# Two layers of a Mamba block gated by a mixture of experts: predicated copies for the first layer's expert, silu in groups of four on ScalarE in the second

## The chip, the cores and the metric

The kernel runs on one core of one Trainium2 chip. The time is device microseconds of one launch. The core has five engines that run side by side and meet at semaphores: TensorE (PE; its weight loads are PEld), VectorE (DVE), ScalarE (ACT), GpSimd (POOL) and SyncE (SP), which here issues all the DMAs.

## The reference, cut to what matters

Input x is 8 x 256 x 128. Both layers compute x = x + s(xn) * silu(ffn(xn)), where xn is the layer norm of x.

```python
# layer 0: ffn, top-1 of 8 experts, each 128 -> 512 -> 128
#   p = softmax(xn @ Wr + br); e = argmax(p)      (for each token)
#   y = p[e] * (relu(ln(xn) @ W1[e] + b1[e]) @ W2[e] + b2[e])
# layer 1: ffn, all 8 experts, weighted
h = jax.nn.silu(x @ w_gate[e]) * (x @ w_up[e])
out = sum_e cw[e] * (h @ w_down[e])   # cw: product of two softmaxes, normalised
# s: Mamba. xc = conv(x @ W_in); gate = silu(xc) (layer 0: times z)
#   delta = softplus(... + b);  state = exp(delta * A) * state + (delta * u) * B;  y = sum_n state * C
# layer 1: y = (y + xc * D) * silu(z) @ W_out, 256 inner channels, 16 states
```

## The kernel before

The 2048 tokens are four pairs of sequences, T = 512 tokens each; a pair goes through layer 0, then (all four done) through layer 1. Tiles are 128 partitions (channels) by 512 tokens, fp32.

A pair has 32 *units* (8 experts x 4 slices of 128 hidden channels), and its work is cut into 32 *slots*, one for each unit. Every engine's program is written out in the order of slots; a loop over pairs runs from slot 6 of one pair to slot 5 of the next, so slots 0 to 5 also hold the *late* part of the pair before. The engines are not otherwise tied: each walks through its own list and waits for semaphores. In a slot stand:

- the unit. `three_passes` forms a hidden tile in one of two PSUM banks (bank2, bank3) out of a high and a low part of weights and input (L1384 to L1386). Layer 0: `hidden0` adds a fourth product, `big` (2^100 on a diagonal, bf16) times `ohm` (one-hot minus 1) at L1426, so that tokens of other experts come out hugely negative; ScalarE's relu with bias (`rectify`, L1186) makes them zero; `down0` (L1444) adds every unit into bank1, two slots later. Layer 1: ScalarE takes tanh of half the gate (`half_gate`, L1225), VectorE multiplies (tanh + 1) by the gate (`finish_gate`, L739, tile gg), TensorE's `up1` (L1496) fills the single bank5 a slot later, VectorE multiplies both (`finish_hidden`, L747, tile hid), and `down1` (L1504) follows three slots later. Before its up product, TensorE waits for the hidden step that frees bank5;
- a *chunk*: one of 16 (layer 0) or 32 (layer 1) state indices. ScalarE forms decay = exp(delta * A) (L1179, ring of four), VectorE drive = dx * B (L612) and the scan over tokens (`tensor_tensor_scan`, L619), POOL multiplies by C and adds (L898 to L923), TensorE sums with the identity (L1397, L1405). B and C come as rows broadcast over partitions by DMA (tile CB, ring of four), each loaded when POOL is done with the chunk four back;
- steps of the *head* of the next pair, given by the tables `HEAD0` and `HEAD1` (slot: names). Each engine has its own part of a step: stat1, var1 and xn are the layer norm, xnT its transposes on TensorE and their copy on ScalarE (L1116), xi0 and xi1 the convolution products (L1359), xs0 and xs1 their silu, z and tz/sz the gate of the block, row and dt the products for B, C and delta, then softplus in parts (ln is a Ln with a table load on each side, L1146 and L1147), lmax, lexp, pick or soft the routing, cwT the experts' weights. All head products share bank7, and each waits until the one before has been read;
- the tail of layer 0's own pair (`TAIL0`): y, yn1, yn2, yn, ynT, s in slots 27 to 31.

In the late part layer 0 adds the experts' biases (L1485), copies bank1 (L1213), transposes it and takes silu of it by tanh (L1218, L673). In the last pair of layer 0 the head is layer 1's, and the gate weights of layer 1 are loaded and split.

The lines that set the order around the change:

```python
CHUNKS1 = [c if c < 8 else c - 1 for c in range(C1)]      # slot of each chunk's drive; scan one slot later
half_gate(i, u)                                            # ACT, every slot
gate1(i, u + 1) ; down1(i, u - LAG1) ; up1(i, u - 1)       # PE, every slot
scan ; finish_hidden(i, u - 2) ; form_drive ; finish_gate  # DVE, every slot
```

## Time and profile before

| | us |
|---|---|
| median of 3 runs | 913.11 (912.3 to 918.16) |
| profiled execution | 914.93, span 913.1, granted TensorE clock 0.971 |
| TensorE busy | 805.6 (88%) |
| VectorE busy | 682.9 (75%) |
| POOL busy | 490.3 (54%) |
| ScalarE busy | 420.7 (46%) |

The span goes from the first to the last instruction of the profiled execution. Busy shares are means over both layers: layer 0 fills the span up to about 400 us, layer 1 the rest. Records of matmuls overlap, so that TensorE's busy time is more than its work; the distance between the starts of two products tells what one costs. In the timelines "x2" is two instructions of one fp32 product.

### The profile page before, as it was taken

The page shows a single profiled execution, that of the slowest core. Times are in us where ns is not written, and L with a number is a line of the kernel's source. Part 1 is how long each engine was busy: PE and PEld are TensorE (multiplying, and loading weights), DVE is VectorE, ACT ScalarE, POOL GpSimd, SP SyncE. Part 2 cuts the span into 40 slices and gives each one's busy share as a digit, 9 for nine tenths or more (in the row PEclk, how much of TensorE's full clock was granted, in tenths as well). Part 3 has the DMA queues.
Part 4 walks back from the last instruction along what each step waited for, and adds up shares of the span by engine and source line. Part 5 has one row for each costly group of instructions (what it writes and reads, how often), then busy time and mean ns, then how long its engine had stood idle before and what let it go on. Part 6 is the DMA issues. An engine that isn't in the chain of part 4 may idle for free.

```text
span 913.1 us, 10705 instructions
## 1 busy us (share of the span) xinstructions
PE 805.6 (88%) x2312; PEld 383.6 (42%) x2312; DVE 682.9 (75%) x1096; ACT 420.7 (46%) x699; POOL 490.3 (54%) x388
## 2 busy tenths in 40 slices
PE   2858998999899988868998987999887999889997
PEld 1324444444444443333454343544343544344443
DVE  4389359927973845349879897789896889899995
ACT  2744554455455634555334633434542434563341
POOL 0086436634660553225756656656655656757773
PEclk9979999999999989998999999999998999999999
DMA  9265255332523553167744575756565745758771
GB/s 266 57 189 136 89 169 150 104 106 83 161 54 106 150 169 88 31 162 193 186 146 125 131 186 143 187 128 154 143 154 131 178 132 141 176 138 212 189 186 35
DMA packets 85851, 129.28 MB, mean 142 GB/s; under 512 B 7368, under 2 KB 28560, under 8 KB 85808
## 3 DMA queue, kind: packets, MB, share of 16 engines
q1 hardware_dynamic: 85808, 128.85, 53.7%
q14 instruction: 33, 0.27, 0.1%
q8 instruction: 10, 0.16, 0.1%
HBM read 125.35 MB, written 3.47 MB: 141 GB/s over the span
## 4 chain that ended last, share of the span: by engine, by line
PE 30%; DVE 16%; issue 11%; ACT 4%; DMA 3%; POOL 1%; DVEq 1%; SPq 1%; ACTq 0%; POOLq 0%
DVE state L619 6%; PE bank L1496 6%; PE bank L1504 5%; DVE bank L612 3%; PE bank L1359 3%; PE bank L1397 3%; DMA CB<-crow 3%; PE bank L1384 2%; PE bank L1386 2%; PE bank L1444 2%; PE bank L1385 2%; DVE gg L739 2%; PE bank L1314 1%; DVE hid L747 1%; ACT sg L1225 1%
## 5 line engine op out<-in xcount | busy, mean ns | idle before, releaser
L619 DVE TENSOR_TENSOR_SCAN state<-decay,bank 128x512 f32<-128x512 f32 x192 | 232.9, 1213 | 17.5 <-issue 9.1
L1384 PE MATMUL bank<-XH,wh 128*128 128x512 f32 x256 | 176.3, 689 | 25.5 <-DVE gg L739 11.1
L1496 PE MATMUL bank<-xw,wu 128*128 128x512 f32 x256 | 141.9, 637 | 36.5 <-DVE hid L747 36.2
L1179 ACT ACTIVATE decay<-delta,negA 128x510 f32<-128x510 f32 x192 | 135.7, 715 | 42.0 <-DVE state L619 41.7
L1186 ACT ACTIVATE hid<-bank,early 128x512 f32<-128x512 f32 x128 | 87.5, 685 | 142.0 <-PE bank L1444 132.2
L612 DVE TENSOR_TENSOR bank<-bank,CB 128x512 f32<-128x512 f32 x192 | 133.2, 694 | 20.6 <-DMA CB<-crow 11.5
L1444 PE MATMUL bank<-hid,wd 128*128 128x512 f32 x256 | 147.5, 659 | 0.0
L902 POOL TENSOR_TENSOR product<-state,CB 128x512 f32<-128x512 f32 x64 | 81.7, 1276 | 99.9 <-DVE state L619 99.9
L1504 PE MATMUL bank<-hid,wd 128*128 128x512 f32 x256 | 132.4, 600 | 0.0
L1225 ACT ACTIVATE sg<-bank 128x512 f32<-128x512 f32 x128 | 75.7, 592 | 99.9 <-PE bank L1386 99.9
L898 POOL TENSOR_TENSOR product<-state,CB 128x512 f32<-128x512 f32 x64 | 81.6, 1276 | 74.4 <-DVE state L619 44.4
L739 DVE SCALAR_TENSOR_TENSOR gg<-sg,bank 128x512 f32<-128x512 f32 x128 | 86.8, 678 | 36.4 <-ACT sg L1225 36.2
L1386 PE MATMUL bank<-XH,wl 128*128 128x512 f32 x256 | 103.5, 404 | 0.0
L1385 PE MATMUL bank<-XL,wh 128*128 128x512 f32 x256 | 102.8, 402 | 0.0
L1384 PEld LDWEIGHTS bank<-XH,wh 128*128 128x128 f32 x256 | 49.6, 194 | 113.5 <-DVE gg L739 52.5
L1496 PEld LDWEIGHTS bank<-xw,wu 128*128 128x128 f32 x256 | 44.1, 194 | 120.9 <-DVE hid L747 94.0
L919 POOL TENSOR_TENSOR product<-state,CB 128x512 f32<-128x512 f32 x48 | 61.4, 1280 | 61.9 <-DVE state L619 57.6
L747 DVE TENSOR_TENSOR hid<-gg,bank 128x512 f32<-128x512 f32 x128 | 84.7, 662 | 5.9 <-PE bank L1496 3.7
L904 POOL TENSOR_TENSOR product<-product 128x512 f32<-128x512 f32 x64 | 83.7, 1307 | 5.0
L1385 PEld LDWEIGHTS bank<-XL,wh 128*128 128x128 f32 x256 | 49.8, 194 | 37.5 <-issue 36.5
L923 POOL TENSOR_TENSOR product<-product 128x512 f32<-128x512 f32 x48 | 63.2, 1317 | 3.8
L1397 PE MATMUL bank<-product,early 128*128 128x512 f32 x128 | 64.7, 592 | 0.0
(167 smaller groups left out, 922.6 us busy)
## 6 DMA issues: line engine op xcount, KB each, us to landing
CB<-crow SPq DMA_DIRECT2D x256, 256.0 KB, 5.0
CB<-crow SPq DMA_DIRECT2D x64, 512.0 KB, 4.8
cwb<-cwrow SPq DMA_DIRECT2D x32, 256.0 KB, 5.7
wu<-W_dram SPq DMA_DIRECT2D x8, 256.0 KB, 5.3
wd<-W_dram SPq DMA_DIRECT2D x8, 256.0 KB, 5.9
wu<-Wu_dram SPq DMA_DIRECT2D x8, 256.0 KB, 3.6
xw<-Wg_dram SPq DMA_DIRECT2D x8, 256.0 KB, 4.6
wd<-Wd_dram SPq DMA_DIRECT2D x8, 256.0 KB, 5.0
```

Source lines behind the costliest of these rows:

```text
L612: v.tensor_tensor(drive, dx, CB[:, c % ROWS, 1, :], ALU.mult).then_inc(drive_ready.sem, 1)
L619: v.tensor_tensor_scan(state[:, c % RING, :], decay[:, c % RING, :], drive, 0.0, ALU.mult, ALU.add).then_inc(state_ready.sem, 1)
L739: v.scalar_tensor_tensor(out=gg[:, u % 2, :], in0=sg[:, u % 2, :], scalar=1.0, in1=bank[HID_BANK + u % HIDS][:, :], op0=ALU.add, op1=ALU.m ...
L747: v.tensor_tensor(hid[:, u % 2, :], gg[:, u % 2, :], bank[UP_BANK][:, :], ALU.mult).then_inc(hid_ready.sem, 1)
L1179: a.activation(by_batch(decay[:, c % RING, :])[:, :, 1:], by_batch(delta[:, m, :])[:, :, 1:], ACT.Exp, scale=negA[:, c:c + 1]).then_inc(de ...
L1384: t.matmul(dst, wh[:, e, ws], XH[:, :], start=True, stop=False)
L1385: t.matmul(dst, wh[:, e, ws], XL[:, :], start=False, stop=False)
L1386: return t.matmul(dst, wl[:, e, ws], XH[:, :], start=False, stop=stop)
L1397: t.matmul(bank[Y_BANK][:, :], ident[:, :], product[:, e % PRODS, :], start=(k == 0), stop=(k == N // PAIR - 1)).then_inc(summed.sem, 1)
L1444: t.matmul(bank[OUT_BANK][:, :], wd[:, u, :], hid[:, u % 2, :], start=(u == 0), stop=False).then_inc(down_done.sem, 1)
L1496: t.matmul(bank[UP_BANK][:, :], wu[:, e, 128 * f:128 * f + 128], xw[:, e % 2, :], start=True, stop=True).then_inc(up_ps.sem, 1)
L1504: ins = t.matmul(bank[OUT_BANK][:, :], wd[:, u, :], hid[:, u % 2, :], start=(u == 0), stop=(u == UNITS - 1))
```

## The change

Layer 0. The mask product and `ohm` go. Each expert's four down products now form a sum of their own, in bank5 and bank1 by turns, and when an expert's sum is complete VectorE copies it into `yfT` where a mask says that the token is this expert's (`select`, 8 for each pair, in slots 6, 10, ... 30 and slot 2 of the next pair). The masks are the one-hot rows, written to DRAM (`send_mask`, in slot 18) and loaded back broadcast over the partitions (`load_mask`). Bias product and transposes of the late part are joined; the transposes of yn go to bank6.

Layer 1. ScalarE computes silu itself, in a group of four units at every fourth slot, with its table loaded before it and the exponentials' table after it; then the exponentials of the scans of slots 4e+3 to 4e+6. Decay and silu tiles lie in rings of six. TensorE computes the gates two by two, in the first and the last slot of a group. VectorE's `finish_gate`, and its steps for xs and sz, go. `HEAD1` is laid out anew, and hand-over, low part, delta and the first two decays of the next pair move from its slot 0 into slots 29 to 31 of the pair before.

```diff
-HEAD1 = {... 11: "xnT", 12: "xi0", 13: "logits", 14: "lmax", 15: "lexp",
-         16: "xs0 z0 tz0", 17: "sz0 xi1", 19: "xs1", 20: "row0", 21: "z1 tz1 soft1", 22: "sz1",
-         24: "dt0 soft2", 25: "row1 rest0 soft3", 26: "dt1 less0", 27: "cwT rest1", 28: "less1 ln", 29: "xr"}
+HEAD1 = {... 11: "xnT", 12: "logits", 13: "lmax", 14: "xi0 lexp",
+         16: "xs0 z0 sz0", 17: "row0", 18: "xi1 soft1", 20: "xs1 z1 sz1", 21: "row1 soft2", 22: "dt0 soft3",
+         23: "rest0", 25: "dt1 less0 rest1", 26: "cwT less1", 29: "ln hand xr", 30: "low del0", 31: "dec0"}
+DECAYS1 = [[c for c in range(2, C1) if FT * e + 3 <= SCAN1[c] <= FT * e + 6] for e in range(E)]
+PLACE = [k % SIX for k in range(UNITS - FT)] + [0, 1, 4, 5]
...
+            def load_mask(j, e):
+                if j > 0 or e >= CWR:
+                    sp.wait_ge(sel_ready.sem, sel_ready.at0(j, e - CWR + 1))
+                src = cwrow[j % 2, e:e + 1, :].to_broadcast((128, T))
+                sp.dma_start(cwb[:, e % CWR, :], src).then_inc(cw_in[e % CWR].sem, 16)
+            def send_mask(j):
+                sp.wait_ge(*use0(head_read, j, "onehot"))
+                sp.dma_start(cwrow[j % 2, :, :], ohT[:, :]).then_inc(cw_out.sem, 16)
+                sp.wait_ge(cw_out.sem, cw_out.at0(j, 16))
...
-                v.tensor_scalar(ohm[:, :], ohT[:, :], 1.0, None, ALU.subtract).then_inc(ohm_ready.sem, 1)
+            def select(i, e):
+                dve.wait_ge(cw_in[e % CWR].sem, cw_in[e % CWR].at0(i, 16 * (e // CWR + 1)))
+                dve.wait_ge(down_done.sem, down_done.at0(i, FT * e + FT))
+                dve.wait_ge(sel_ready.sem, sel_ready.at0(i, e))
...
+                v.memset(pause[:, e % 2:e % 2 + 1], 0.0)
+                v.copy_predicated(yfT[:, :], cwb[:, e % CWR, :].bitcast(mybir.dt.int32), bank[out_bank(e)][:, :]).then_inc(sel_ready.sem, 1)
...
-            def finish_gate(i, u):
-                v.scalar_tensor_tensor(out=gg[:, u % 2, :], in0=sg[:, u % 2, :], scalar=1.0, in1=bank[HID_BANK + u % HIDS][:, :],
-                                       op0=ALU.add, op1=ALU.mult).then_inc(gg_ready.sem, 1)
-                v.tensor_tensor(hid[:, u % 2, :], gg[:, u % 2, :], bank[UP_BANK][:, :], ALU.mult).then_inc(hid_ready.sem, 1)
+                v.tensor_tensor(hid[:, u % 2, :], sg[:, PLACE[u], :], bank[UP_BANK][:, :], ALU.mult).then_inc(hid_ready.sem, 1)
...
-                half_gate(i, u)
...
+                if u % FT == 0:
+                    silu(i, u)
+                    silu(i, u + 1)
+                    for name in steps_:
+                        if name in ("xs0", "xs1"):
+                            head(name, j)
+                    silu(i, u + 2)
+                    silu(i, u + 3)
...
+                    for c in DECAYS1[u // FT]:
+                        form_decay(i, c)
...
-                three_passes(dst, e, f, False)
-                t.matmul(dst, big[:, e:e + 1].to_broadcast((E, 128)), ohm[:, :], start=False, stop=True).then_inc(hid_ps.sem, 1)
+                three_passes(dst, e, f, True).then_inc(hid_ps.sem, 1)
...
-                t.matmul(bank[OUT_BANK][:, :], wd[:, u, :], hid[:, u % 2, :], start=(u == 0), stop=False).then_inc(down_done.sem, 1)
+                t.matmul(bank[out_bank(e)][:, :], wd[:, u, :], hid[:, u % 2, :], start=(f == 0), stop=(f == FT - 1)).then_inc(down_done.sem, 1)
...
-                if u + 1 < UNITS:
+                if u % FT == 0:
+                    gate1(i, u + 2)
+                    gate1(i, u + 3)
+                if u % FT == FT - 1 and u + 1 < UNITS:
                     gate1(i, u + 1)
+                    gate1(i, u + 2)
```

ScalarE in layer 1 before, from the copy of the transposed input (slot 11) over slot 12; sg is the tanh of a gate, sp_u and sp_l are xi0's two readings:

```order
L1116 ACTIVATE XNP<-bank7 128x2x256 [waits xl_ready,xr_ready]
L1222 REGISTER_ALU
L1224 REGISTER_ALU [waits hid_ps]
L1225 ACTIVATE sg<-bank2 128x512 [waits gg_ready]
L1178 REGISTER_ALU [waits delta_ready]
L1179 ACTIVATE decay<-delta,negA1 128x2x255 [waits state_ready]
L1118 REGISTER_ALU
L1119 ISA [waits head_ps]
L1122 ACTIVATE sp_u<-bank7,early 128x512 [waits delta_ready,sp_l_ready,xs_ready]
L1123 ACTIVATE sp_l<-bank7,early 128x512
```

The same place now (sg is silu):

```order
L1153 ACTIVATE XNP<-bank7 128x2x256 [waits xl_ready,xr_ready]
L1265 REGISTER_ALU
L1267 REGISTER_ALU [waits hid_ps]
L1268 ACT_TABLE_LOAD
L1268 ACTIVATE sg<-bank2 128x512 [waits hid_ready]
L1265 REGISTER_ALU
L1268 ACTIVATE sg<-bank3 128x512 [waits hid_ready,hid_ps]
...
L1218 REGISTER_ALU [waits delta_ready]
L1219 ACT_TABLE_LOAD
L1219 ACTIVATE decay<-delta,negA1 128x2x255 [waits state_ready]
```

One tanh and one exponential a slot have become four silus and up to four exponentials at every fourth slot, with a table load ahead of each kind; here both stand behind the copy of the transposes.

VectorE in layer 0 before, slot 6 from the scan to the first statistics:

```order
L618 REGISTER_ALU [waits drive_ready,decay_ready]
L619 SCALAR_TENSOR_TENSOR state<-decay,bank4 128x512 [waits state_used]
L638 REGISTER_ALU
L639 COPY szm<-ohT 8x512 [waits mix_ps]
L641 TENSOR_SCALAR hp<-linv 128x4
L534 ISA
L500 BN_STATS stats<-xt 128x6 [waits x_in]
```

And now; cwb is the mask, bank5 the sum of expert 0:

```order
L669 REGISTER_ALU [waits drive_ready,decay_ready]
L670 SCALAR_TENSOR_TENSOR state<-decay,bank4 128x512 [waits state_used]
L637 ISA
L638 ISA [waits cw_in0]
L639 ISA [waits down_done]
L641 REGISTER_ALU [waits sel_ready]
L642 MEMSET pause 128x1 [waits yf_ps]
L643 COPY_PREDICATED yfT<-cwb,bank5 128x512
L693 COPY szm<-ohT 8x512 [waits yf_ps]
L695 TENSOR_SCALAR hp<-linv 128x4
L579 ISA
L545 BN_STATS stats<-xt 128x6 [waits x_in]
```

The copy, with its wait for the mask's DMA and for TensorE's fourth down product, stands ahead of the head's statistics, and one like it at every fourth slot.

TensorE in layer 0, two units before:

```order
L1384 MATMUL bank2<-XH,wh 128x512 [waits hid_ready]
L1385 MATMUL bank2<-XL,wh 128x512
L1386 MATMUL bank2<-XH,wl 128x512
L1426 MATMUL bank2<-ohm,big 128x512
L1444 MATMUL bank1<-hid,wd 128x512 [waits hid_ready,wd_in1]
L1422 REGISTER_ALU
L1384 MATMUL bank3<-XH,wh 128x512 [waits hid_ready]
L1385 MATMUL bank3<-XL,wh 128x512
L1386 MATMUL bank3<-XH,wl 128x512
L1426 MATMUL bank3<-ohm,big 128x512
L1444 MATMUL bank1<-hid,wd 128x512 [waits hid_ready]
```

and now:

```order
L1432 MATMUL bank2<-XH,wh 128x512 [waits hid_ready]
L1433 MATMUL bank2<-XL,wh 128x512
L1434 MATMUL bank2<-XH,wl 128x512
L1487 ISA [waits wd_in1]
L1489 MATMUL bank1<-hid,wd 128x512 [waits hid_ready,sel_ready]
L1470 REGISTER_ALU
L1432 MATMUL bank3<-XH,wh 128x512 [waits hid_ready]
L1433 MATMUL bank3<-XL,wh 128x512
L1434 MATMUL bank3<-XH,wl 128x512
L1489 MATMUL bank1<-hid,wd 128x512 [waits hid_ready]
```

The mask product is gone from every unit, and an expert's first down product waits for the copy of the expert two before, whose bank it takes.

## Rows read from the trace of the kernel before

**Rows 1.** The page, busy time of each engine.
```profile
PE 805.6 (88%) x2312; PEld 383.6 (42%) x2312; DVE 682.9 (75%) x1096; ACT 420.7 (46%) x699; POOL 490.3 (54%) x388
```

**Rows 2.** Stretches: us, busy PE, PEld, DVE, ACT, POOL; layer 0 (1, 3), layer 1.
```profile
125.70:210.20 84.50, 81.04 (x250) 38.19 (x250) 57.79 (x104) 44.27 (x71) 41.89 (x33) 0.98 0.38 110
294.80:403.10 108.30, 95.63 (x275) 44.07 (x275) 56.00 (x95) 54.40 (x91) 41.94 (x33) 0.94 0.39 110
529.50:661.40 131.90, 117.84 (x329) 57.31 (x329) 111.24 (x165) 57.98 (x99) 79.96 (x63) 0.97 0.62 152
791.60:895.60 104.00, 97.69 (x276) 48.24 (x276) 100.85 (x138) 41.86 (x70) 75.48 (x60) 1.00 0.74 180
```

**Rows 3.** Timeline of TensorE, layer 1: start, us, engine, line, operation, tiles.
```profile
577.64 0.39 PE L1385 MATMUL bank<-XL,wh 128*128 128x512 f32 x1
...
578.10 1.02 PE L1504 MATMUL bank<-hid,wd 128*128 128x512 f32 x2
578.96 1.02 PE L1496 MATMUL bank<-xw,wu 128*128 128x512 f32 x2
```

**Rows 4.** Timeline of VectorE over the same slot.
```profile
576.71 1.22 DVE L619 TENSOR_TENSOR_SCAN state<-decay,bank 128x512 f32<-128x512 f32 x1
...
578.42 0.69 DVE L612 TENSOR_TENSOR bank<-bank,CB 128x512 f32<-128x512 f32 x1
579.02 0.68 DVE L739 SCALAR_TENSOR_TENSOR gg<-sg,bank 128x512 f32<-128x512 f32 x1
579.61 1.21 DVE L619 TENSOR_TENSOR_SCAN state<-decay,bank 128x512 f32<-128x512 f32 x1
```

**Rows 5.** Chain that ended last, layer 1, pair 1: start, us, what.
```profile
544.69 1.79 PE bank L1541 x16
...
590.39 1.69 PE bank L1367 x16
```

**Rows 6.** Timeline of TensorE, layer 1, with [idle before <-releaser].
```profile
559.14 2.08 PE L1496 MATMUL bank<-xw,wu 128*128 128x512 f32 x2 [3.65 <-DVE hid L747]
...
656.76 0.50 PE L1384 MATMUL bank<-XH,wh 128*128 128x512 f32 x1 [1.29 <-DVE gg L739]
```

**Rows 7.** Timeline of TensorE, layer 0, a slot with nothing beside the unit.
```profile
140.10 1.12 PE L1444 MATMUL bank<-hid,wd 128*128 128x512 f32 x2
...
141.53 0.40 PE L1386 MATMUL bank<-XH,wl 128*128 128x512 f32 x1
141.86 0.39 PE L1426 MATMUL bank<-ohm,big 8*128 8x512 bf16 x1
142.18 1.13 PE L1444 MATMUL bank<-hid,wd 128*128 128x512 f32 x2
```

**Rows 8.** Busy time by stretch, layer 0, pair 1, slots 4 to 20.
```profile
137.40:183.90 46.50, 43.59 (x133) 20.49 (x132) 43.66 (x75) 22.12 (x36) 29.72 (x24) 0.96 0.45 123
```

**Rows 9.** Timelines, layer 0, pair 1: g, TensorE's wait for xn, yn.
```profile
136.87 0.69 DVE L673 SCALAR_TENSOR_TENSOR yfT<-yfT,bank 128x512 f32<-128x512 f32 x1 [3.04 <-ACT yfT L1218]
...
154.87 0.66 PE L1309 MATMUL bank<-early,xn 128*128 128x128 f32 x4 [2.42 <-DVE xn L513]
...
201.93 1.36 DVE L513 TENSOR_SCALAR so<-bank,mv,rstd_t 128x128 f32<-128x128 f32 x4 [1.20 <-POOL rstd_t L869]
```

**Rows 10.** Timeline of ScalarE around its Ln, layer 1.
```profile
519.64 1.28 ACT L1146 ACT_TABLE_LOAD   x1
520.94 1.06 ACT L1146 ACTIVATE sp_l<-sp_u 128x1024 f32<-128x1024 f32 x1
522.01 1.28 ACT L1147 ACT_TABLE_LOAD   x1
...
523.42 0.58 ACT L1225 ACTIVATE sg<-bank 128x512 f32<-128x512 f32 x1
```

**Rows 11.** The page, DMA issues: tiles, count, KB each, us to landing.
```profile
CB<-crow SPq DMA_DIRECT2D x256, 256.0 KB, 5.0
```

**Rows 12.** Groups by line: busy us, mean ns | idle before, releaser.
```profile
L747 DVE TENSOR_TENSOR hid<-gg,bank 128x512 f32<-128x512 f32 x128 | 84.7, 662 | 5.9 <-PE bank L1496 3.7 <-PE bank L1504 2.2
```

More of the change, by code:

```diff
@@ L45 @@
 RING = 4
+SIX = 6
 HIDS = 2
@@ L50 @@
 LAG0, LAG1 = 2, 3
+SELECT_AT = FT + LAG0
 GROUP = 4
@@ L123, with freed @@
 BANK1 = [s for s in steps(HEAD1) if s in "xnT xi0 xi1 logits z0 z1 cwT row0 dt0 row1 dt1".split()]
+def freed(k, pair):
+    earlier = [n for n in range(k) if PLACE[n] == PLACE[k]]
+    if earlier:
+        return max(earlier) + 1
+    if isinstance(pair, int) and pair == 0:
+        return 0
+    return max(n for n in range(UNITS) if PLACE[n] == PLACE[k]) + 1 - UNITS
 class Signal:
@@ L728, in head1 @@
                     rounding(m, sp_u_ready.at1(j, m + 1))
+                if name == "low":
+                    if not first_pair(j):
+                        low1(j)
+                if name == "del0":
+                    form_delta(lambda signal, n: signal.at1(j, n), 0, J1, decay_ready.at1(j, 0 if first_pair(j) else -N))
             def low1(i):
@@ L1144, in head1 @@
                 if name == "ln":
-                    act.wait_ge(sp_u_ready.sem, sp_u_ready.at1(j, J1))
+                    act.wait_ge(sp_c_ready.sem, sp_c_ready.at1(j, J1))
                     a.activation(sp_l[:, :, :], sp_u[:, :, :], ACT.Ln).then_inc(sp_l_ready.sem, 1)
                     a.activation(warm[:, :], ones[:, :], ACT.Exp)
+                if name == "hand" and not first_pair(j):
+                    hand_over1(j)
+                if name == "dec0":
+                    for c in range(2):
+                        form_decay(j, c)
                 if name in ("dt0", "dt1"):
@@ L1245, in slot1 @@
                     keep(i)
-                if head:
-                    for name in now(HEAD1, u):
+                for name in steps_:
+                    if name not in ("xs0", "xs1", "sz0", "sz1"):
                         head(name, j)
@@ L1482, in late0 @@
                     down0(i, UNITS - LAG0 + u)
[L1483 removed]
+                if u == 3:
+                    pe.wait_ge(sel_ready.sem, sel_ready.at0(i, E))
                     pe.wait_ge(ohF_ready.sem, ohF_ready.at0(i, 1))
[L1485 to L1487 removed]
+                    pe.wait_ge(head_read.sem, head_read.at0(PAIRS, 0) + len(BANK1) if i is PAIRS - 1 else head_read.at0(i + 2, 0))
+                    for k in range(TT):
+                        here = slice(128 * k, 128 * k + 128)
+                        t.matmul(hb[:, here], yfT[:, here], ident[:, :], start=True, stop=False)
+                        last = t.matmul(hb[:, here], ohF[:, here], b2[:, :], start=False, stop=True)
+                    last.then_inc(yf_ps.sem, 1)
             def up1(i, u):
```

205 lines of the change are left out of this document (101 added, 104 removed).

## The prediction

> **What bounds the kernel now.** I read the busy shares first, then the table of stretches, then the two timelines of TensorE and VectorE side by side, and the waits last.
>
> TensorE is busy 88% of the span and VectorE 75% [rows 1], but the two layers differ. One pair of layer 0 takes 84.5 us with VectorE busy 57.8 of them; one pair of layer 1 takes 131.9 us with VectorE busy 111.2 [rows 2]. Busy time of TensorE is inflated by overlapping records, so I use the distance between starts: an fp32 product of 512 columns costs 0.86 us (578.10 to 578.96) and one of the three gate passes 0.23 us (577.64 to 578.10 is two) [rows 3]. A unit of layer 1 is thus 3 x 0.23 + 0.86 (up) + 0.86 (down) = 2.41 us, plus a sum of 0.86 every second unit: 2.84 us. In the same slot VectorE goes scan, hidden, drive, gate: scan to scan is 2.90 us (576.71 to 579.61) [rows 4]. So the two engines are equally loaded, each waits in turn for the other, and whatever the head of the next pair adds to one of them is paid in full. A pair of layer 1 holds, on TensorE: 32 x 2.41 = 77.1; 16 sums x 0.86 = 13.8; the head's 14 large fp32 products x 0.86 = 12.0; logits 1.7 and output projection 1.8 [rows 5]; three sets of transposes, about 1.3: in all 107.7 us. Observed 131.9, so 24 us are loss: waits for VectorE (up to 3.65 us at once, and 1.29 for the gate) and the half clock after the long one, where two halves took 2.08 us and not 1.02 [rows 6, 3].
>
> In layer 0 a unit with nothing beside it takes 2.08 us (140.10 to 142.18) [rows 7]: from the third pass to the down product 0.65 (141.53 to 142.18), where layer 1 has 0.23, and about 0.1 more behind the down product. Without the mask product I expect layer 1's 0.69 + 0.86 = 1.55. But from slot 4 to slot 20 VectorE is busy 43.7 of 46.5 us [rows 8], and TensorE waits 2.42 us there for xn [rows 9]: in half of each layer-0 pair VectorE is the bound.
>
> **Layer 1, part by part.** Removed on VectorE: 32 gate steps whose pitch is 0.59 (579.02 to 579.61 [rows 4]) = 19 us of a pair, and four steps for xs and sz, some 3. VectorE's slot falls from 2.90 to 2.31, under TensorE's 2.84. TensorE becomes the only bound. The gates now come two slots together (both at a group's first and last slot), so TensorE's distances between two up products are 3.96, 1.72, 2.58, 3.10 us. In the 1.72 gap VectorE finishes its hidden step late by 0.6 us, but the next gap of 2.58 takes that up; I cost it at nothing, and at 0.6 x 8 = 5 us a pair if it does not.
>
> Added on ScalarE: 16 table loads a pair. The load starts at 519.64, the Ln behind it at 520.94, the next load at 522.01 as that Ln ends [rows 10]: 1.30 us each, 20.8 a pair. ScalarE was busy 58.0 of 131.9 [rows 2]; less the two steps for each of xi0 and xi1 (four of 0.7, 2.8) it comes to 76, of some 122. It is covered as long as it comes to a group's first silu in time: TensorE computes that gate a slot early and has 2.4 to 3.3 us of gate, down, up (and sum) before it needs the bank again, against 1.30 + 0.6 (523.42 [rows 10]) on ScalarE. The cover is missing where a head step stands directly ahead: xnT in slot 11, copied by ScalarE only after TensorE's last product of the slot, then a load, then silu(12): 0.1 + 0.6 + 1.3 + 0.6 = 2.6 us in which TensorE stands. The softplus of dt0 before silu(24) and hand-over, low and gate at slots 29 to 31 I put at 1 us each. Behind each late silu stand the decays, row and dt copies on ScalarE; the scans need the decays three slots later, which hides them. CB loads take 5.0 us to land [rows 11] in a ring of four; after row1 the loads are queued on SP behind its two writes, and with faster slots I allow 1 us.
>
> The sum for a pair with a head: 107.7 + 5.4 (the stop near 559 with its slow clock [rows 6]; it falls where the loop over pairs jumps back, and I let it stay) + 1.7 (a second slow stretch) + 2.6 + 2 + 1 + about 3 of small gaps = 123.4, against 131.9: 8.5 less, three times, 25.5. The last pair has no head: 104.0 us for its 32 slots [rows 2], of which TensorE needs 93; with 5 of small losses 98, 6 less. Its tail after the last scan stays. Layer 1: -31.5.
>
> **What the Trainium skill says of the loads.** "ScalarE: Activation LUTs", section "What ACT_TABLE_LOAD costs", gives about 1.28 us for the load and about 1.38 us of drain, 2.66 in all for a switch. The trace disagrees: the Ln began 0.02 us after its load ended and the load 0.01 us after the work before it [rows 10]. By the page ScalarE would carry 22 us more a pair, some 98 of 122, and the second rival below would be likely; by the row it has room.
>
> **Layer 0, part by part.** Removed on TensorE: 0.52 us x 32 = 16.7 a pair. Added on VectorE: 8 copies. The trace has no predicated copy. The nearest row by its operands (one in PSUM, one in SBUF) is hidden, 0.66 us [rows 12]; the dearest 512-column step is the scan, 1.21 [rows 4]. I take 0.7 with 0.1 for the memset and the waits in front, and keep 0.5 to 1.3 for the range. Also gone: the step for ohm, 0.3.
> Slots 0 to 18, VectorE's half: its wait of 3.04 us for g in slot 4 [rows 9] shrinks by 2.2, as TensorE arrives 4 x 0.52 sooner; three copies ahead of the expert choice cost 2.4; ohm gives 0.3. About nothing is gained (-0.1), and TensorE's gift of 0.52 a slot becomes a longer wait at xnT.
> Slots 19 to 31, TensorE's half: 13 x 0.52 = 6.8 less. The copy of expert 6 stands before yn in slot 30 and waits for a product of slot 29: 0.7 + 1.4 (yn [rows 9]) + 0.1 against a slot of 1.55 gives back 0.7; the chain y, stats, variance, yn, which has three slots of 1.55 instead of 2.08, I cost at 0.3: -5.8. The mask's DMAs (8 x 256 KB a pair) are queued on SP between the CB loads, and wait for a copy two experts back, which VectorE has passed by then; the one wait that blocks SP, the landing of the mask rows in slot 18, comes after the last CB load of the pair. I cost them at nothing; 1 us a pair if they delay CB.
> Pairs 1 and 2: -5.9 each. Pair 0 -4.5 (irregular start, and the first mask row is queued before the first rows). Pair 3 took 108.3 us [rows 2] and carries layer 1's first head: 20 slots behind xnT x 0.52 = -10.4, -0.6 before it, and +4.5 for four table loads in it, which hold up relu, on which TensorE waits with only 0.6 us of slack. Together -6.5. Layer 0: -22.8.
>
> **Sum.** -31.5 - 22.8 = -54.3 us. The profiled execution took 914.9 us (span 913.1 and 1.8 around it), so 860.6; the median of the runs shown is 1.8 lower: 859.
>
> **The rivals.**
> A. Layer 0 gives little: the predicated copy costs 1.2 or more, and the copies tie VectorE to TensorE. Then its half grows by 3 x 0.5, the tail by 0.5, pair 3's head by 3: layer 0 gives -12 and not -22.8. For it: VectorE's 43.7 of 46.5 us. Against: in the other half it is nearly idle. Time 870; with small losses in layer 1 up to 880.
> B. ScalarE becomes the bound in the head groups: each load costs twice the row (the page's price), the six groups with head steps of a pair lose 1.5 to 2 us each, about 11 x 3 = 33 us. Time 892. Against: the rows of the four loads show no such gap.
> C. Layer 1 gains more: the small gaps and the second slow stretch go with VectorE's waits, pairs at 116 us: 3 x 7 less. Time 838.
> D. Slower than before: TensorE waits at every group for silu. The place is the first silu of a group, behind the decays of the group before, each of which waits for the scan six chunks back. If ScalarE arrives after its whole train (4 decays x 0.6 + 2 loads x 1.3 = 5.0 us) while TensorE has 2.4 of other work, 2.6 us are lost in each of 32 groups, 83 us: 859 + 83 = 942. It decides from 1.7 us a group on (54 / 32). Against: the scan waited for is that of the group's first slot, done before the silus are.
>
> **How the numbers follow.** The forecast (845 to 869) has 0.47, A 0.20, B 0.10, C 0.16, D 0.07. The low end of the range is C, 838; the high end has to hold A and most of B, 892; what is left out is half of C's outer side, D and a little of B. A measurement of this kernel tells about 1% from no change. Faster by over 1% hold the forecast, A, C and nearly all of B: 0.90; within 1%: 0.04, slower: 0.06, from D and its milder forms.
>
> **What would show it.** In the changed trace: VectorE busy below 90 us of a layer-1 pair and pairs of about 123 us; silu groups with two loads of 1.28 each and ScalarE near 76 us a pair; TensorE waiting for ScalarE at slot 12 and hardly elsewhere; the predicated copy near 0.7 us; layer-0 pairs of 78 to 79 us with a longer wait at xnT than 2.42. The prediction is wrong if TensorE waits for silu in groups without head steps, if layer-1 pairs stay at 130, or if the layer-0 pair loses all of 16 us (then VectorE was no bound there).

## The result and the profile after

The changed kernel takes 924.13 us (median of 13 runs), the kernel before, on the same chip, 915.0 (13 runs): ratio 1.0086, 95% interval 1.0059 to 1.0114. I had forecast 859 in a range of 838 to 892. The profiled execution took 922.94 us (span 921.1). Two of the changed kernel's 13 executions (933.0 and 933.9 us) fell in a slower state of the chip and do not enter the ratio; the median of the other eleven is 923.0. The change did what it says on VectorE and ScalarE, and the time did not fall: it rose by 0.9%.

The busy times answer to [rows 1]:

```profile
PE 769.3 (84%) x2224; PEld 411.0 (45%) x2224; DVE 626.4 (68%) x1013; ACT 506.3 (55%) x755; POOL 485.3 (53%) x388
```

TensorE has 36 us less, VectorE 57 us less, ScalarE 86 us more. Now the table of stretches (us, busy PE, PEld, DVE, ACT, POOL, granted clock, DMA share, GB/s), which answers to [rows 2]: layer 0 pairs 1 and 3, then layer 1 pair 1 and the last pair.

```profile
125.00:210.00 85.00, 71.99 (x229) 42.08 (x228) 63.92 (x119) 43.45 (x70) 41.87 (x33) 0.90 0.47 138
295.00:403.00 108.00, 85.13 (x256) 47.00 (x257) 60.38 (x108) 60.05 (x95) 42.35 (x34) 0.91 0.47 132
527.60:665.20 137.60, 119.48 (x328) 60.74 (x328) 92.13 (x128) 79.17 (x115) 78.71 (x62) 0.94 0.58 144
802.00:906.00 104.00, 98.46 (x278) 51.10 (x278) 86.70 (x107) 63.48 (x86) 75.07 (x59) 0.98 0.71 178
```

The third line runs from one low part (tile XL) of layer 1 to the next, one whole period of the order. VectorE fell from 111 to 92 us in such a pair and ScalarE stands at 79, both within 3 us of the forecast; the pair lasts 137.6 us, where it lasted 131.9. The clock column moved too: 0.98 became 0.90 in layer 0, 0.97 became 0.94 in layer 1.

**Layer 0.** Timelines of VectorE, TensorE and ScalarE at the start of pair 1 (start, us, engine, line, operation, tiles, [idle before <-releaser]); they answer to [rows 9]:

```profile
130.36 0.73 DVE L643 COPY_PREDICATED yfT<-cwb,bank 128x512 f32<-128x512 int32 x1
138.87 0.69 DVE L729 SCALAR_TENSOR_TENSOR yfT<-yfT,bank 128x512 f32<-128x512 f32 x1 [5.88 <-ACT yfT L1261]
```

```profile
131.22 0.48 PE L1536 MATMUL bank<-early,yfT 128*128 128x128 f32 x2 [1.37 <-DVE yfT L643]
...
134.22 0.79 PE L1537 MATMUL bank<-b,szm 8*128 8x128 f32 x2
134.94 2.08 PE L1489 MATMUL bank<-hid,wd 128*128 128x512 f32 x2
```

```profile
137.12 0.69 ACT L1232 ACTIVATE hid<-bank,early 128x512 f32<-128x512 f32 x1 [6.49 <-PE bank L1489]
137.70 1.13 ACT L1261 ACTIVATE yfT<-bank,hp 128x128 f32<-128x128 f32 x4
```

Read them backwards. VectorE waits 5.88 us for g, where it waited 3.04. ScalarE's tanh (L1261) came at 137.70 although its input was complete at 134.94: in ScalarE's order it stands behind relu 3 (L1232), which waits for a down product (L1489) that TensorE has behind the joined block. That block of eight short products took 3.7 us, behind a stop of 1.37 us for the copy of expert 7 (L643). Its length is not the half clock: the granted clock was 1.00 in its first half and 0.74 in its second, and stood at 0.50 (1.2 GHz) only behind it, from 135 us on:

```profile
131.20:133.00 1.80, 1.78 (x9) 1.30 (x10) 1.69 (x2) 0.00 (x0) 1.72 (x2) 1.00 0.73 193
133.00:135.00 2.00, 2.00 (x9) 1.31 (x9) 0.00 (x0) 0.00 (x0) 1.68 (x3) 0.74 0.74 251
135.00:138.00 3.00, 3.00 (x6) 1.77 (x6) 0.00 (x0) 0.88 (x3) 0.97 (x1) 0.50 0.93 159
```

The half clock stretched the down product and the unit behind it (the down product took 2.08 us and not 1.02). Cut at the marks XL, g, onehot and next XL in both traces, pair 1 was 12.0 + 37.3 + 35.3 = 84.6 us and is 14.9 + 39.8 + 30.5 = 85.2.

**Layer 1.** All stops of TensorE over 0.3 us in one period of pair 1 (timeline, 535 to 668 us); they answer to [rows 6]:

```profile
541.51 1.13 PE L1548 MATMUL bank<-xw,wu 128*128 128x512 f32 x2 [1.96 <-DVE hid L786]
558.12 2.08 PE L1548 MATMUL bank<-xw,wu 128*128 128x512 f32 x2 [4.17 <-DVE hid L786]
576.43 1.13 PE L1548 MATMUL bank<-xw,wu 128*128 128x512 f32 x2 [2.99 <-DVE hid L786]
587.15 0.50 PE L1432 MATMUL bank<-XH,wh 128*128 128x512 f32 x1 [2.73 <-ACT sg L1268]
637.22 0.50 PE L1432 MATMUL bank<-XH,wh 128*128 128x512 f32 x1 [0.41 <-ACT sg L1268]
649.72 2.08 PE L1548 MATMUL bank<-xw,wu 128*128 128x512 f32 x2 [4.05 <-DVE hid L786]
666.07 0.49 PE L1432 MATMUL bank<-XH,wh 128*128 128x512 f32 x1 [1.64 <-DVE XL L779]
```

Before, thirteen such stops made 13.6 us in such a pair, only one of them over 1.5 us; now seven make 18.0, five of them over 1.9. The one of 4.05 us is new. VectorE and ScalarE just ahead of it:

```profile
647.27 0.69 DVE L574 SCALAR_TENSOR_TENSOR sp_e<-sp_u,sp_e 128x512 f32<-128x512 f32 x1 [5.13 <-ACT sp_u L1102]
```

```profile
644.65 0.69 ACT L1098 ACTIVATE sp_e<-bank,early 128x512 f32<-128x512 f32 x1 [1.27 <-PE bank L1362]
...
646.61 0.63 ACT L1102 ACTIVATE sp_u<-sp_e 128x512 f32<-128x512 f32 x1
```

That is step rest1. The new `HEAD1` puts it in slot 25, the slot of dt1 itself, so VectorE stands until TensorE's product and ScalarE's four steps are through, with the next scan and the next hidden step behind it. Before, rest0 stood in the slot after dt0, and rest1 one slot after dt1.

### The profile page after: what moved, and what is told of

It is laid out like the page before. It is cut to its first block and busy times, and to the rows that moved or that the text cites. A ratio compares the mean times of both kernels' runs of the same rounds, so it can differ in the third digit from the quotient of the medians.

```text
span 921.1 us, 10560 instructions
## 1 busy us (share of the span) xinstructions
PE 769.3 (84%) x2224; PEld 411.0 (45%) x2224; DVE 626.4 (68%) x1013; ACT 506.3 (55%) x755; POOL 485.3 (53%) x388
## 5 line engine op out<-in xcount | busy, mean ns | idle before, releaser
L1432 PE MATMUL bank<-XH,wh 128*128 128x512 f32 x256 | 175.4, 685 | 27.6 <-ACT sg L1268 10.7
L1548 PE MATMUL bank<-xw,wu 128*128 128x512 f32 x256 | 139.9, 629 | 40.9 <-DVE hid L786 40.4
L1232 ACT ACTIVATE hid<-bank,early 128x512 f32<-128x512 f32 x128 | 86.9, 684 | 134.0 <-PE bank L1489 125.5
L1489 PE MATMUL bank<-hid,wd 128*128 128x512 f32 x256 | 144.7, 649 | 0.0
L786 DVE TENSOR_TENSOR hid<-sg,bank 128x512 f32<-128x512 f32 x128 | 86.2, 673 | 77.9 <-PE bank L1548 74.0
L1219 ACT ACTIVATE decay<-delta,negA 128x510 f32<-128x510 f32 x192 | 126.9, 710 | 7.7 <-DVE state L670 4.5
L1433 PE MATMUL bank<-XL,wh 128*128 128x512 f32 x256 | 109.4, 427 | 0.0
L1434 PE MATMUL bank<-XH,wl 128*128 128x512 f32 x256 | 108.7, 425 | 0.0
L1548 PEld LDWEIGHTS bank<-xw,wu 128*128 128x128 f32 x256 | 46.5, 196 | 117.5 <-DVE hid L786 73.0
L1432 PEld LDWEIGHTS bank<-XH,wh 128*128 128x128 f32 x256 | 53.8, 210 | 91.0 <-issue 48.6
L1433 PEld LDWEIGHTS bank<-XL,wh 128*128 128x128 f32 x256 | 53.9, 211 | 39.8 <-issue 36.3
L1557 PEld LDWEIGHTS bank<-hid,wd 128*128 128x128 f32 x256 | 48.7, 193 | 36.9 <-issue 30.1
```

Source lines behind the costliest of these rows:

```text
L786: v.tensor_tensor(hid[:, u % 2, :], sg[:, PLACE[u], :], bank[UP_BANK][:, :], ALU.mult).then_inc(hid_ready.sem, 1)
L1219: a.activation(by_batch(decay[:, PLACE[c], :])[:, :, 1:], by_batch(delta[:, m, :])[:, :, 1:], ACT.Exp, scale=negA[:, c:c + 1]).then_inc(de ...
L1232: a.activation(hid[:, u % 2, :], bank[HID_BANK + u % HIDS][:, :], ACT.Relu, bias=col0("b1", u)).then_inc(hid_ready.sem, 1)
L1432: t.matmul(dst, wh[:, e, ws], XH[:, :], start=True, stop=False)
L1433: t.matmul(dst, wh[:, e, ws], XL[:, :], start=False, stop=False)
L1434: return t.matmul(dst, wl[:, e, ws], XH[:, :], start=False, stop=stop)
```

## The experiments

Medians, and marks read from each profiled execution: the time of layer 1's first low part, which stands at the same place in every kernel (the end of layer 0), and three pairs of layer 1, from VectorE's first hidden step of the first pair to that of the last. The later low parts are no common mark, as the new `HEAD1` moves them from slot 0 to slot 30 of the pair before. "Clock" is the median over the runs of the mean granted clock. The runs were made on several chips; the kernel before took 914.2 to 915.9 us beside them, and each ratio is to its own chip's.

| kernel | median us | clock | layer 0 ends | three pairs of layer 1 |
|---|---|---|---|---|
| before | 915.0 | 0.969 | 402.3 | 392.6 |
| changed | 924.1 | 0.934 | 400.7 | 406.5 |
| layer0_alone | 910.7 | 0.951 | 399.2 | 395.5 |
| layer1_alone | 940.5 | 0.946 | 412.6 | 410.7 |
| down_ahead_of_join | 917.1 | 0.935 | 391.1 | 410.7 |
| bias_ahead | 912.3 | 0.940 | 389.6 | 407.0 |
| three_copies_left_out | 922.9 | 0.938 | 398.1 | 409.0 |
| rest1_later | 905.1 | 0.936 | 398.6 | 392.5 |
| xnT_a_slot_earlier | 891.9 | 0.946 | 402.6 | 375.3 |
| silu_table_early | 901.0 | 0.943 | 403.9 | 387.4 |
| filled_stops | 900.1 | 0.953 | 401.1 | 387.3 |
| rest1_and_layer0_order | 889.3 | 0.949 | 390.7 | 389.2 |
| all_orders | 876.6 | 0.952 | 387.5 | 379.2 |
| all_orders_again | 876.3 | 0.954 | 386.4 | 375.6 |
| all_orders_filled | 875.8 | 0.958 | 386.5 | 371.6 |
| filled_at_two_stops | 873.7 | 0.964 | 388.6 | 370.0 |

One profiled execution is not a median: the changed kernel, down_ahead_of_join, bias_ahead and three_copies_left_out have the same order in layer 1, and its three pairs took 406.5 to 410.7 us.

### Each part by itself

The first kernel is the one before with the copies, masks and joined product of layer 0; the second has the silu groups and the new table of layer 1.

> The kernel before with the change of layer 0 alone (predicated copies, masks, joined bias product). Theory: in the changed kernel every layer-0 pair takes as long as before (85.0 against 84.5 us), and layer 1 does not depend on layer 0; so the time is that of before, 915 (912 to 918), with the wait for g in slot 4 near 5.9 us and not 3.0. Rival: layer 0 gains something that is lost again only in the pair that carries layer 1's new head; then pair 3 is shorter than 105 us and the time is 905 to 911.

> The kernel before with the change of layer 1 alone (silu in groups on ScalarE, new head table). Theory: it carries the whole loss: 923 (920 to 926), pairs of layer 1 of 132 to 134 us. Rival: the two parts get in each other's way (clock, DMA); then this part alone is at 915 or below.

Measured: 910.72 us, ratio to before 0.9952 (0.9923 to 0.9982), and 940.52 us, ratio 1.0309 (1.0254 to 1.0363). Layer 0's change is worth 4 us (2 to 7 by the interval), in the range of the rival: pairs 0 to 2 end at 293.8 us (294.0 before), and pair 3 takes 105.4 us (108.3). VectorE's wait for g is 5.5 us, as the theory had it. Layer 1's change costs 25 us alone, far more than expected, and only 13 beside layer 0's (924.1 less 910.7). Some 8 of these 12 us of difference lie in the last pair of layer 0, which carries layer 1's first head: it grows by 8.9 us alone, from 108.3 to 117.2, and by 1 beside layer 0's change, from 105.4 to 106.4. Its stretch and the two new stops of TensorE in layer1_alone:

```profile
295.40:412.60 117.20, 101.06 (x275) 47.39 (x274) 55.01 (x93) 61.27 (x97) 41.61 (x33) 0.89 0.37 104
```

```profile
352.57 2.07 PE L1328 MATMUL bank<-XNP,later 128*128 128x512 f32 x2 [3.45 <-ACT xs L1121]
...
370.65 1.13 PE L1328 MATMUL bank<-XNP,later 128*128 128x512 f32 x2 [1.98 <-ACT xs L1121]
```

A head product (z0 in slot 16, z1 in slot 20) waits there until ScalarE has loaded silu's table and read the bank, and the clock of the stretch is 0.89. In the changed kernel the same stops (3.59 and 1.98 us) fall in a pair that has lost its mask products: 106.4 us.

### rest1 in a slot of its own

```diff
-         23: "rest0", 25: "dt1 less0 rest1", 26: "cwT less1", 29: ...
+         23: "rest0", 25: "dt1 less0", 26: "cwT", 27: "rest1 less1", 29: ...
```

> The changed kernel with step rest1 (VectorE, in layer 1's head) in slot 27 and not in slot 25 beside dt1, cwT alone in slot 26, less1 in slot 27. Theory: VectorE's 5.1 us wait for ScalarE's sp_u goes, with it TensorE's stop of 4.05 us and some 2 us of half clock behind it: 5 us in each of three pairs, 908 to 912. Rival: the delay only moves to the chain rest, less, ln, delta at the pair's end, and the stop comes back at slot 31 or 0: 922 to 926.

Measured: 905.05 us, ratio to before 0.9876 (0.9803 to 0.9948): 19 us less than the changed kernel, with an uncertainty of 7 (four runs), more than expected. The step stands in four heads and not three, as the last pair of layer 0 carries one of layer 1's. In the profiled executions layer 1's pair 1 fell from 137.6 to 133.8 us and pair 2 from 136.6 to 129.1. The step now runs without a wait:

```profile
645.61 1.18 DVE L574 SCALAR_TENSOR_TENSOR sp_e<-sp_u,sp_e 128x512 f32<-128x512 f32 x1
```

The stop of 4.05 us is gone from TensorE's timeline and has not come back elsewhere in the pair. One name in a table of slots costs more than the whole difference between the two kernels. The next three kernels, rest1_and_layer0_order and the four kernels of the last comparison have this edit too.

### xnT a slot earlier

```diff
-HEAD1 = {6: "stat1", 7: "var1", 9: "xn", 11: "xnT", ...
+HEAD1 = {6: "stat1", 7: "var1", 9: "xn", 10: "xnT", ...
```

> The kernel rest1_later with xnT in slot 10 of layer 1's head and not 11. Theory: ScalarE's copy and the table load are done before the gate of slot 12 is; the stop of 2.73 us at slot 12 and about 1.5 us of half clock behind it go in three pairs: 905 - 11 = 894 (890 to 899). Rival: xn itself is late in slot 10, the stop comes a slot earlier and is longer: 905 to 910.

Measured: 891.87 us, ratio 0.975 (0.9691 to 0.9809), as expected. ScalarE's copy and load now come early enough:

```profile
573.51 0.60 ACT L1153 ACTIVATE XNP<-bank 128x512 f32<-128x512 f32 x1 [4.12 <-PE bank L1357]
574.46 1.28 ACT L1268 ACT_TABLE_LOAD   x1 [0.36 <-PE bank L1434]
575.76 1.08 ACT L1268 ACTIVATE sg<-bank 128x512 f32<-128x512 f32 x2
```

The stop of 2.73 us is gone from the timeline. The 13 us between the medians (four runs each) have an uncertainty of some 9, too much to split them into the stop and what follows it. The profiled executions can be split: pair 1 fell by 7.3 us, from 133.8 to 126.5, of which TensorE's stops are 4.1 (this one, and 1.1 from the one at slot 9) and its products 3.2. Slower products behind the stop are a part of it: in the changed kernel the down product there (589.24) lasts 1.91 us where it else lasts 1.02.

### The table load off the path

```diff
                 for name in steps_: ...
+                if u % FT == FT - 1:
+                    a.activation(early_silu[:, u // FT:u // FT + 1], ones[:, :], ACT.Silu)
```

> The kernel rest1_later with a silu of one column at the end of every fourth slot of ScalarE, so that the table load does not wait for the group's first gate. Theory: ScalarE has room, the load leaves the path from gate to silu (1.28 us a group), but TensorE waits for silu only at slots 12, 24 and 0: 2 to 4 us in all, 901 to 903. Rival, that table loads on the path from gate to silu hold up TensorE at every group: 10 us or more, 895 or below.

Measured: 901.03 us, ratio 0.9833 (0.9772 to 0.9893), 4 us less than rest1_later, but the two intervals overlap: with four runs each this gain is not shown. The load now ends before the gate is there:

```profile
555.40 1.28 ACT L1298 ACT_TABLE_LOAD   x1
556.69 0.20 ACT L1298 ACTIVATE early_silu<-ones 128x1 f32<-128x1 f32 x1
560.58 1.31 ACT L1268 ACTIVATE sg<-bank 128x512 f32<-128x512 f32 x2 [3.69 <-DVE hid L786]
```

What decides against rival D of the prediction, and against the rival of this run, is the list of stops above: of pair 1's seven, two wait for silu (sg), 2.73 us behind xnT and 0.41 at another group. In all 32 groups of the changed kernel TensorE's products waited for silu 7 times, 10.7 us together. The loads cost little where no head step stands ahead of them.

### Stops filled with products

```diff
+            def fill(count):
+                for k in range(count):
+                    t.matmul(bank[OUT_BANK][:, :], nought[:, :], XH[:, :].bitcast(F32), start=False, stop=False)
...
+                if u == 12 and head:
+                    fill(3)
...
+                if u == 6 and head:
+                    fill(4)
```

> The kernel rest1_later with products by zero added to the sum in bank1, which change nothing in it: four (0.86 us each) in slot 6 ahead of the up product that waits 4.29 us, three in slot 12 ahead of the gate that waits 2.73 us, in the three pairs with a head. Theory: TensorE then never stops there, its clock stays at 2.4 GHz, and the 6 us and 4 us of half clock behind the two stops go: some 3 + 1.5 us in each of three pairs, so 905 - 13 = 892 (888 to 897), mean granted clock from 0.93 to 0.96. Rival: the half clock has another cause, then the clock stays at 0.93 and the time at 905 or above.

Measured: 900.11 us, ratio 0.9815 (0.9756 to 0.9874), against 905.05 for rest1_later: 5 us, not 13, and the two intervals overlap, so that the gain is not shown. The clock rose from 0.936 to 0.953, most of what was expected. TensorE in slot 6 of layer 1, pair 1:

```profile
556.43 3.60 PE L1563 MATMUL bank<-XH,nought 128*128 128x512 f32 x8
560.79 1.12 PE L1549 MATMUL bank<-xw,wu 128*128 128x512 f32 x2 [0.76 <-DVE hid L786]
561.35 0.80 PE L1433 MATMUL bank<-XH,wh 128*128 128x512 f32 x1
561.99 0.40 PE L1434 MATMUL bank<-XL,wh 128*128 128x512 f32 x1
```

The up product behind the stop lasts 1.12 us (2.08 without the filling), the gate's passes 0.40 (0.63): 2.4 GHz and not 1.2. TensorE is sooner at slot 9, and there it waits 2.62 us for VectorE, which lacks its CB rows: part of the gain turns into the next wait.

### Layer 0: who holds up g

```diff
                 hidden0(i, u)
+                if u == 3:
+                    down0(i, u - LAG0)
                 if u > 0 and late:
                     late(u)
-                if u >= LAG0:
+                if u >= LAG0 and u != 3:
                     down0(i, u - LAG0)
```

> The changed kernel; in slot 3 of layer 0 TensorE issues the down product of unit 1 ahead of the joined bias product and transposes. Theory: ScalarE's tanh for g stands behind relu 3, which waits for that down product; with it first, tanh can start when the joined product ends, 2 to 3 us earlier, VectorE's wait for g falls from 5.9 to about 3 us, and as VectorE is the bound from there to slot 19 the three pairs give 2 to 3 us each: 915 to 918. Rival: the half clock makes the joined product itself the whole delay; then the tanh starts no earlier and the time stays at 924.

Measured: 917.12 us, ratio to before 1.0017 (0.9991 to 1.0042), 7 us less than the changed kernel. The tanh starts right behind the joined block, and VectorE's wait is halved.:

```profile
132.38 1.14 ACT L1261 ACTIVATE yfT<-bank,hp 128x128 f32<-128x128 f32 x4 [3.24 <-PE bank L1539]
```

```profile
133.55 0.69 DVE L729 SCALAR_TENSOR_TENSOR yfT<-yfT,bank 128x512 f32<-128x512 f32 x1 [2.93 <-ACT yfT L1261]
```

The block itself still takes 3.4 us (128.85 to 132.27), at a granted clock of 1.00 in its first half and 0.92 in its second, so the rival's half clock is not what makes it long.

The next kernel also issues the four bias products ahead of the wait for the copy, so that only the transposes stand behind it:

```diff
+                    for k in range(TT):
+                        t.matmul(hb[:, here], ohF[:, here], b2[:, :], start=(k == 0), stop=False)
                     pe.wait_ge(sel_ready.sem, sel_ready.at0(i, E))
                     for k in range(TT):
-                        t.matmul(hb[:, here], yfT[:, here], ident[:, :], start=True, stop=False)
-                        last = t.matmul(hb[:, here], ohF[:, here], b2[:, :], start=False, stop=True)
+                        last = t.matmul(hb[:, here], yfT[:, here], ident[:, :], start=False, stop=(k == TT - 1))
```

> The kernel down_ahead_of_join, with the four bias products issued ahead of the wait for the last predicated copy and the four transposes behind it. Theory: the joined block of 3.7 us behind the copy shrinks to the transposes (1.0 us, or less at full clock), TensorE's stop of 1.4 us is filled, g is ready 2 us earlier in each of four pairs: 917 - 7 = 910 (907 to 913). Rival: something else sets g by now (relu 3 or the decays ahead of the tanh on ScalarE); then at most 1 us a pair, 914 or above.

Measured: 912.31 us, ratio 0.9953 (0.9923 to 0.9982). In pair 1 the bias products take 1.1 us and the transposes 0.9, without a stop between them, and the wait for g is 1.12 us. The same sixteen halves took 3.4 us in down_ahead_of_join, where a transpose (128 partitions) and a bias product (8) take turns, and 2.0 us here, sorted by kind, both at or near full clock. Of the 7 us expected 5 came.

In the third, rest1_later has the first of these edits, and VectorE's step for g stands in slot 5 and not 4:

> The kernel rest1_later with the edit of down_ahead_of_join, and with VectorE's step for g in slot 5 and not 4. Theory: the gains of the two parts add, 905 - 7 = 898, and g a slot later lets VectorE do a drive and a scan (1.9 us) in the wait: another 1.9 x 3 = 5 us, 893 (889 to 898). Rival: what layer 0 gains does not show because layer 1 starts in another position and clock: 900 or above.

Measured: 889.26 us (four runs, 882.6 to 895.7), ratio 0.9688 (0.9614 to 0.9761), as expected: edits of the two layers add, within that spread.

### The copies themselves

```diff
+                if e < 3:
+                    v.memset(nil[:, e:e + 1], 0.0).then_inc(sel_ready.sem, 1)
+                else:
                     v.copy_predicated(...).then_inc(sel_ready.sem, 1)
```

> The changed kernel without the predicated copies of experts 0, 1 and 2 (a memset of one column stands in their place, so the results of these experts are left out). Theory: VectorE is the bound from slot 4 to slot 19 of layer 0, so each copy is paid in full there, 3 x 0.61 = 1.8 us in each of three pairs and a little in the fourth: 924 - 6 = 918 (916 to 920). Rival: TensorE with its half clock is the bound there; then the time stays at 922 to 925.

Measured: 922.89 us, ratio 1.0061 (1.0028 to 1.0093): 1.2 us less than the changed kernel by the medians, 2.3 by the ratios with an uncertainty of some 4, where 6 were expected. The time lies in the rival's range, but its reason does not hold: VectorE has no gap over 0.3 us from g to onehot, so TensorE is not the bound there; yet from g to onehot pair 1 took 38.9 us in place of 39.8, where three copies of 0.61 us are gone: 0.9 us of 1.8. VectorE and POOL in slot 6:

```profile
144.53 0.41 DVE L697 COPY szm<-ohT 8x512 f32<-8x512 f32 x1
...
144.86 1.27 DVE L699 TENSOR_SCALAR hp<-linv 128x4 f32<-128x4 f32 x1
```

```profile
144.85 1.27 POOL L956 TENSOR_TENSOR product<-state,CB 128x512 f32<-128x512 f32 x1 [0.91 <-DVE state L674]
```

A step over four columns, 0.15 us in the changed kernel, takes 1.27 here, exactly as long as POOL's product beside it. Pulled forward by the missing copy, it met POOL; this meeting costs 0.28 us net of one that the changed kernel has at the copy ahead of it, and a second one, at the variance in slot 11 (from 0.19 to 0.63 us), 0.44: together 0.7 of the missing 0.9. Layer 0 ends 2.6 us sooner in the profiled execution (398.1 against 400.7), and layer 1, in which nothing was edited, takes 2.5 us more (409.0 against 406.5): the medians cannot settle a difference of this size.

### All orders together, and the clock again

all_orders has rest1, xnT, the early table load, the down product and the bias products ahead, and g in slot 5. all_orders_filled adds `fill(4)` in slot 6, filled_at_two_stops also `fill(2)` in slot 9.

> The changed kernel with the edits of rest1_later, xnT_a_slot_earlier, silu_table_early, down_ahead_of_join, g in slot 5, and bias_ahead. Theory: they stand at different places and add: 905 - 13 (xnT) - 4 (table) - 16 (layer 0) - 4 (bias) = 868 (862 to 876). Rival: they share waits (VectorE's or POOL's), and each takes part of what the other would give: 878 or above.

> The kernel all_orders with four products by zero in slot 6 of layer 1 ahead of the up product that waits for VectorE's first scan behind the jump. Theory: as in filled_stops the clock stays at 2.4 GHz behind it, 2.6 us in each of three pairs, of which the wait at slot 9 gives back half: 3 to 5 us less than all_orders. Rival: what TensorE gains is spent in a longer wait for CB rows at slot 9: within 2 us of all_orders.

Measured: 876.62 us, ratio to before 0.957 (0.9537 to 0.9604), and 875.76 us, 0.9573 (0.954 to 0.9607). The orders give 47 us against the changed kernel and 38 against the one before. They do not quite add: the time is 9 us over the sum of 868, just outside the 862 to 876 that was expected. The filling made no difference by these medians, though by the profiled executions 7.6 us. So both were measured once more side by side:

> The kernel all_orders once more, beside the next on one chip, since the medians of all_orders and all_orders_filled lay 0.9 us apart while their profiled executions lay 7.6 us apart. Theory (the half clock has a price of its own): 877 to 879 with a mean clock of 0.950 to 0.952, 4 us above the next. Rival (the clock is bought with the added products and gives nothing): within 1 us of the next.

> The kernel all_orders_filled with two more products by zero in slot 9 of layer 1, ahead of the up product that waits 2.6 us there. Theory: mean clock 0.960 or more, and 3 to 6 us under all_orders_again: 871 to 874. Rival: no difference, 876 to 878, in spite of the higher clock.

Measured: 876.3 us (six runs, 874.3 to 880.9), ratio 0.9581 (0.9552 to 0.9609), and 873.74 us (six runs, 872.1 to 874.9), ratio 0.9551 (0.9529 to 0.9573). The intervals of the ratios overlap. The twelve times themselves, taken on one chip, differ by 3.3 us in the mean with an uncertainty of 2.7, so there is a gain, and a small one; by the medians it is 2.6 us. The time lies in the theory's 871 to 874. Layer-1 pairs 1 and 2, first all_orders_again, then filled_at_two_stops:

```profile
502.90:630.40 127.50, 116.31 (x328) 59.55 (x328) 92.72 (x129) 80.22 (x123) 79.00 (x62) 0.96 0.62 157
630.40:756.20 125.80, 114.75 (x328) 58.62 (x328) 92.74 (x129) 80.13 (x122) 79.03 (x62) 0.97 0.60 158
```

```profile
507.00:630.50 123.50, 117.35 (x340) 58.98 (x340) 92.93 (x129) 80.19 (x122) 79.04 (x62) 1.00 0.67 162
630.50:752.80 122.30, 117.08 (x340) 59.00 (x340) 91.65 (x129) 80.15 (x122) 79.06 (x62) 1.00 0.64 164
```

TensorE's timeline splits a pair into stops, added products and the kernel's own products. Pair 1 was 11.0 us of stops and 116.5 of products; filled it is 5.8 of stops, 5.3 of added products and 112.3 of its own. Pair 2 went from 11.0 + 114.8 to 5.0 + 5.3 + 112.0. The filling takes the time of the stops it fills, and the products between them run 2.8 to 4.2 us faster with the clock at 2.4 GHz throughout: that is the slow clock's own price in these two executions. The three pairs last 123.3 us each there (370.0 by 3).

## Why the prediction was wrong, point by point

- **What each operation costs: right.** The predicated copy takes 0.736 us (median of 32; 0.61 from its start to the next step's) where I took 0.7; the layer-0 unit on TensorE 1.55 us; VectorE 92 us in a layer-1 pair (below 90 forecast), ScalarE 79 (76 forecast). The table loads:

```profile
585.21 1.28 ACT L1268 ACT_TABLE_LOAD   x1
586.50 1.09 ACT L1268 ACTIVATE sg<-bank 128x512 f32<-128x512 f32 x2
...
590.10 1.28 ACT L1219 ACT_TABLE_LOAD   x1
```

  The silu starts 0.01 us after its load: 1.29 us each, as read from [rows 10], and no drain of 1.38 us as the Trainium skill has it ("ScalarE: Activation LUTs", "What ACT_TABLE_LOAD costs"). Rival B is out.
- **The term "g shrinks by 2.2": wrong, the failed step of layer 0.** I let the wait for g shrink because TensorE "arrives sooner". I followed one engine and not the chain copy of expert 7, joined block, down product, relu 3, tanh. From XL to g the pair grew by 2.9 us in place of shrinking by 2.5 (g and ohm): 5.4 us a pair. The other terms held: three copies and what goes with them +2.5 (I had +2.4) between g and onehot; the tail from onehot on -4.8 (I had -5.8). Their sum, +0.6 a pair, is what the trace shows, where I had -5.9. Pair 0 fell by 0.7 us and not by 4.5. down_ahead_of_join and bias_ahead, which cut that chain alone, gave 12 us.
- **The sum of a layer-1 pair, 107.7 + 15.7 = 123.4: the failed step of layer 1, too small in its stops, its work and its slow clock.** Pair 1 took 137.6 us, pair 2 136.6. By TensorE's timeline pair 1 is 17.9 us of stops and 119.7 of products. The sum had 12.3 of stops (3.7 of the 5.4, 2.6, 2, 1 and 3) and 111.1 of products (107.7 and 3.4 for the slow clock).
  - Stops, 5.6 us short. The 2.6 us at slot 12 (2.73) were right. Left out was rest1, a head step moved into the slot of the product it waits for, with its stop of 4.05 us: the diff shows it, and "the softplus ... I put at 1 us each" priced only silu 24 behind it. The small gaps were not 3 us but 1.96 + 2.99 (hidden behind VectorE's steps at the pair's start, and CB rows at slot 9).
  - Work, 4.6 us short. In filled_at_two_stops, at a granted clock of 1.00, the kernel's own products take 112.3 us of pair 1 and not 107.7. Which item of the sum was short was not followed.
  - "Slow clock, 5.4 + 1.7", 4 us short: 119.7 less 112.3 is 7.4, where I had 3.4. I gave the half clock to two places; in pair 1 it stands behind four stops, of 4.17, 2.99, 2.73 and 4.05 us. The kernel before has some 5.8 us of it in such a pair by the same reckoning (131.9 less 13.8 of stops less 112.3), so the change added little slow clock there and 4 us of stops. In the 11 executions of the ratio the changed kernel's time goes with the mean clock, from 918.9 us at 0.941 to 929.5 at 0.925; that is no proof of cause, since a longer stop does both.
- **Pair 3, -6.5: too much.** It fell by 1.9 us, from 108.3 to 106.4. The part that failed is not the +4.5 for the table loads: layer 1's change costs 1 us there beside layer 0's (8.9 alone). It is the -11.0 for the mask products, of which layer0_alone shows 3: TensorE takes up xn 3.5 us later in the pair than before and not 0.6 sooner (it waits 6.11 us there and not 3.30), and the slots behind it give 6.4 us of the 10.4. What held back the other 4 was not followed. I had looked at relu behind the loads and not at z0 and z1, whose products wait 3.59 and 1.98 us for ScalarE to read the shared bank7.
- **The rivals.** D had the right sign for the whole, by another mechanism: TensorE waits for silu at groups with a head step ahead of them, and hardly elsewhere. A and C gave no account of it. None of the rivals was a head step put a slot too near to what it waits for.
- **What the change could give.** With the orders put right the layer-1 pairs last 123 to 126 us on average (370.0 and 375.6 by 3), where I had forecast 123.4, and the kernel takes 874 to 876, where I had 859. That the pair comes so near is in part luck: its products alone take 112 us at full clock where I had 107.7, and its stops come to 11 us with their filling, where I had 12.3 and 3.4 of slow clock.

## What to carry to other kernels

When a hand-written order is laid out anew, walk through every moved step and ask in which slot its input is made and what stands behind it on its engine: one step in the slot of its own product cost about 19 us here (12 to 26), twice what the whole change lost. A freed engine shortens nothing while a chain over three engines (copy, product, activation queued behind another) sets the next start. And a stop of TensorE can cost more than its length, by the slower products behind it; count that from rows, since here it was a few us of a pair and the stops themselves were more.
